# Attention values on TensorE moved from the end of a slot to directly behind the transposed scores

## What is computed

```
# layer 0 (cross): adaptive layer norm of x and of the context
q = xq @ Wq + bq ;  k, v = split(xkv @ Wkv + bkv)
x = x + softmax(q k^T / 4) v @ Wp + bp
# layer 1 (self)
h = layer_norm(x) * (1 + scale_msa) + shift_msa
x = x + (mha(h) @ self_o_w + self_o_b) * gate_msa
# layer 2 (cross), keys and values of the raw context
x = x + mha(layer_norm(x) @ q_w + q_b, context) @ cross_o_w + cross_o_b
# MLP
h = layer_norm(x) * (1 + scale_mlp) + shift_mlp
x = x + (gelu(h @ mlp_w1 + mlp_b1) @ mlp_w2 + mlp_b2) * gate_mlp
```

## Time and profile before

| | |
|---|---|
| median of 3 runs | 520.54 us |
| the profiled execution | 521.28 us |
| its span on the core, first to last instruction | 519.5 us |
| mean granted TensorE clock | 0.930 of 2.4 GHz |
| busy share PE, DVE, ACT, POOL | 85%, 56%, 48%, 35% |

### The profile page before, as it was taken

The page is one execution under the profiler, slowest core; times in us unless marked ns, Lnnn a source line. Parts: engine busy times, 40 slices in busy tenths (PEclk is TensorE's granted clock), DMA queues, the critical chain, the costliest instruction groups (busy, mean ns, idle before and its releaser), DMA issues.

```text
span 519.5 us, 11670 instructions
## 1 busy us (share of the span) xinstructions
PE 441.9 (85%) x4306; PEld 314.7 (61%) x4306; DVE 293.0 (56%) x784; ACT 249.5 (48%) x555; POOL 183.2 (35%) x245
## 2 busy tenths in 40 slices
PE   4767199888999989889697786899999998999996
PEld 3634156657576556566564553576666665689995
DVE  7648176693757565533757686556754574434321
ACT  1442147654574556445442433466666664562221
POOL 3343033463345345516214314235243422252200
PEclk9968589998899999989987997799999998999999
DMA  7899934295425188936817205238456241200000
GB/s 216 195 132 168 161 78 117 67 188 99 54 62 113 33 127 126 123 89 78 98 51 94 55 3 137 89 84 105 85 81 102 58 88 48 73 3 18 20 18 19
DMA packets 48927, 46.13 MB, mean 89 GB/s; under 512 B 12767, under 2 KB 47071, under 8 KB 48871
## 3 DMA queue, kind: packets, MB, share of 16 engines
q1 hardware_dynamic: 45951, 45.12, 47.1%
q10 hardware_dynamic: 2920, 0.27, 0.5%
HBM read 14.57 MB, written 0.93 MB: 30 GB/s over the span
## 4 chain that ended last, share of the span: by engine, by line
PE 58%; DVE 18%; issue 8%; DMA 6%; ACT 5%; POOL 3%; SPq 2%; ACTq 0%; DVEq 0%; POOLq 0%
DVE nmax L940 9%; PE bank L451 7%; PE bank L593 7%; PE bank L573 6%; PE bank L459 6%; PE bank L556 6%; PE bank L644 5%; PE bank L485 5%; PE bank L633 5%; DMA q_stack_all<-nm_t 3%; PE bank L618 3%; DVE xn L841 2%; ACT prob L785 2%; PE bank L508 2%; PE bank L468 1%
## 5 line engine op out<-in xcount | busy, mean ns | idle before, releaser
L940 DVE TENSOR_REDUCE nmax<-bank 112x1 f32<-112x375 f32 (+1 forms) x288 | 141.8, 547 | 88.1 <-PE bank L556 86.7
L785 ACT ACTIVATE prob<-bank 128x448 f32<-128x448 f32 (+2 forms) x224 | 113.4, 544 | 76.3 <-PE bank L573 72.1
L556 PE MATMUL bank<-k_stack,q_stack_all 96*128 96x375 bf16 x256 | 67.2, 342 | 14.9 <-DVE nmax L940 6.4
L573 PE MATMUL bank<-q_stack_all,k_stack 99*128 99x112 bf16 x768 | 56.4, 218 | 14.4 <-DMA q_stack_all<-nm_t 14.3
L1079 POOL TENSOR_TENSOR fill_space<-fill_space 128x375 f32<-128x375 f32 x32 | 30.2, 946 | 105.6 <-ACT fill_space L717 105.6
L573 PEld LDWEIGHTS bank<-q_stack_all,k_stack 99*128 99x128 bf16 x768 | 42.1, 100 | 32.2 <-DMA q_stack_all<-nm_t 15.1
L593 PE MATMUL bank<-prob,v_tokens 128*17 128x112 f32 (+1 forms) x1536 | 57.5, 267 | 0.1
L1093 POOL TENSOR_TENSOR v_tokens<-v_tokens,bias_rows_v 128x256 f32<-128x256 f32 (+1 forms) x48 | 33.4, 711 | 57.9 <-ACT v_tokens L729 57.7
L556 PEld LDWEIGHTS bank<-k_stack,q_stack_all 96*128 96x128 bf16 x256 | 24.3, 101 | 48.3 <-DVE nmax L940 26.4
L451 PE MATMUL bank<-fill_space,wkv 128*128 128x375 f32 x128 | 51.0, 527 | 1.7 <-ACT fill_space L738 1.7
L459 PE MATMUL bank<-wkv,fill_space 128*128 128x256 f32 (+1 forms) x192 | 48.5, 389 | 2.4 <-DVE v_all L911 1.6
(11 more groups left out here) (120 smaller groups left out, 676.2 us busy)
## 6 DMA issues: line engine op xcount, KB each, us to landing
k_stack<-fill_space SPq DMA_DIRECT2D x192, 93.8 KB, 3.7
q_stack_all<-q_part SPq DMA_DIRECT2D x72, 112.0 KB, 4.1
k_stack_all<-ctx_norm SPq DMA_DIRECT2D x24, 112.0 KB, 5.4
k_stack_all<-in_L_xcond_mlp_w_dram SPq DMA_DIRECT2D x2, 1024.0 KB, 7.1
k_stack_all<-in_L_xcond_ada_w_dram SPq DMA_DIRECT2D x1, 1536.0 KB, 16.6
ctx_tokens<-in_ctx_dram SPq DMA_DIRECT2D x2, 512.0 KB
fill_space<-gate_rows SPq DMA_DIRECT2D x2, 448.0 KB, 3.6
fill_space<-gate_rows SPq DMA_DIRECT2D x1, 896.0 KB, 5.2
```

The source lines that it names most:

```text
L556: last = pe.matmul(to[:, o:o + w], q_all[0:DEEP, q + h * N2:q + h * N2 + P], keys, start=True, stop=True)
L573: last = pe.matmul(bank[SCORE_T[n % 2]][:, j * T:(j + 1) * T], keys, q_all[0:AUG, q + h * N2:q + h * N2 + T], start=True, stop=True)
L785: act.activation(prob[n % 4][0:rows, :], bank[SCORE_T[n % 2]][0:rows, 0:GH * T], ACT.Exp).then_inc(exp_done, 1)
L940: dve.tensor_reduce(nmax[:, g * hs:(g + 1) * hs], bank[SCORE[n % 3]][0:T, 0:hs * w].rearrange("t (h k) -> t h k", k=w), AX_X, ALU.max, neg ...
```

## The change

In `tensor`, the loop of PE over slots issues the values directly behind the transposed scores and the steps last. Nothing is added or removed, and no other engine's program changes.

```
                 for u in units:
                     pe_scores_t(pe, a, u)
+                if v > 0:
+                    for u in (v - 2, v - 1):
+                        pe_values(pe, a, u)
                 for u in (v, v + 1):
                     for step in STEPS.get((a, u), ()):
                         pe_step(pe, step)
-                if v > 0:
-                    for u in (v - 2, v - 1):
-                        pe_values(pe, a, u)
```

## The result

The changed kernel takes 528.22 us, the median of 4 runs (526.37 to 528.74), against 520.58 us for the kernel before, run beside it (4 runs, 518.55 to 522.02). The ratio is 1.0148 with a 95% interval of 1.011 to 1.0186: 1.5% slower, 7.6 us. The forecast was 527.6. The profiled execution of the changed kernel took 528.58 us, its span is 526.8 us at a mean granted clock of 0.935; before it was 521.28, 519.5 and 0.930.

A forecast was written before the change was run, and what follows sets the result against it. PE, busy for 85% of the span, was taken to bound the kernel. Terms 6.3 + 2.7 + 0.5 - 3.7 + 1.3 = +7.1 us on 521.28 gave 528.4, or 527.6 on the median's scale; range 519.5 to 533.

The forecast's parts named there:

- Term 1: Ends of cross items: values 11 wait for exponential 11 behind T's copy; nine exposed ends at 0.70 us, +6.3 us.
- term 4: Given back: values moved into existing PE waits, in items 1 to 3, 5, 6, 22 and 23; -3.7 us together.
- Term 2: Start of next item: tail transposes L606 wait for ACT's `pv_sb` copy, 0.22 or about 0.4 us each; +2.7 us.
- term 3: Start of item 8: PE waits for the maxima's DMA, whose N step stands one pair later; +0.5 us.
- Term 5: Self items: output projection L618 now comes behind values 3, which wait for exponential 3; gains and losses sum to +1.3 us.
- (a): Rival: ends cost less, first layer's swallowed by DVE's chain, item 22 avoids the slow clock; 523.0 us, chance 0.20.
- (b): Rival: not slower, as five clock falls in items 6, 9, 11, 16 and 22 go; 518.6 us, chance 0.10.
- (c): Rival: much slower, the clock falls at three to nine item ends, 1.8 us each; 533 to 544 us, chance 0.10.

The follow-up runs named there:

- the control: The kernel before, PE's order unchanged, with step T of place 10 put at place 11, so ACT does exponential 11 before T's copy: 526.62 us, ratio 1.0102.
- after again: A second profiled execution of the changed kernel, with nothing altered: 529.56 us.
- both repairs: Changed kernel with T of place 10 at place 11 and `pv_sb` ahead of the last place's steps on ACT: 521.51 us; self items in old order: 521.19.

## Why the prediction was right, step by step

**Term 1, the ends.** The mechanism is shown. Values 11 wait for exponential 11, which stands behind the copy of the first T; the version with the last slots alone has it, changing ACT's order removes it (2.49), and the control turns its sign. The size was 0.80 instead of 0.70 an end. The wait itself was placed to 0.05 us (values 11 at 2.55 behind scores 10, forecast 2.50); the other 0.05 is in values 11 and the second T, 0.70 against 0.65. In the first layer the wait is 0.87, longer by its longer copy (0.18), but before, the second T waited 0.24 us there, and the end of item 0 is 3.43 instead of 2.64: 0.79 more, so that this cancels as worked out. Item 4's end, which I had as hidden, shows the same 0.79; the wait for keys behind it gives that back (2.08 before, 1.26 now), and of the pair of term 4 only 0.15 is left to see in item 5 (0.22 longer, against 0.37 with the last slots alone).

**Term 2, `pv_sb`.** The mechanism is shown by moving that copy alone, and the term was undersized: 0.43 to 0.46 us an item in the last layer instead of 0.22, and in the first layer 0.50 in item 1 (L606 at 81.33, the scores at 79.94, against 0.89 before) and 0.60 in items 2, 4, 5 and 6 instead of 0.4. 0.21 of it lies between the end of `pv_sb` (408.14) and the start of L606 (408.35). I had set that distance at 0.05, as between an exponential and its values. The version with the last slots alone holds terms 1 and 2 (the N step of term 3 stands in an earlier slot). Its cross items are 11.1 us longer where I had 9.0, although items 6 and 7 are 0.3 and 0.8 shorter there, with no fall of the clock in item 6.

**Term 3, item 8's start.** Item 7 is 0.83 and 0.77 longer, forecast 0.5. PE at its end still waits for the DMA of the maxima:

```profile
249.56 0.66 PE L573 MATMUL bank<-q_stack_all,k_stack_all 99*128 99x112 bf16 x8 [0.56 <-DMA q_stack_all<-nm_t]
```

From the N step to these scores it is 4.96 us before and 4.95 now, so item 8 starts as late as N does, as forecast, and the wait of 0.51 us ahead of values 11, which I hadn't put there, lies inside that time and costs nothing. But N stands 0.83 us later in its item (20.71 to 21.54), not 0.51. A fall of the clock reaches 2.4 us into item 7 before and 2.9 now; whether that is the rest wasn't tested.

**Term 4, given back.** The cross items are together 6.8 and 8.0 us longer in the two executions of the changed kernel, and 11.1 longer with the last slots alone. So all the rest of the change gives -4.3 and -3.1, where my terms 3 and 4 make -3.2, but its places were partly others. In item 1 I foresaw no wait ahead of the last S and a smaller one ahead of N. The changed kernel shows them almost as they were in the earlier trace rows:

```profile
90.01 0.79 PE L556 MATMUL bank<-k_stack,q_stack_all 96*128 96x375 bf16 x2 [0.34 <-DVE nmax L940]
...
94.70 0.21 PE L524 MATMUL bank<-ident_bf,nparts 112*128 112x112 bf16 x1 [0.68 <-DVE nparts L952]
```

Item 1 is 0.67 longer and the pair's gain is still in it, since with the last slots alone it is 1.30 longer: -0.63 where I had -0.51. That the waits nonetheless stay, where the pair was to fill them, is not due to the late L606: with `pv_sb` moved, L606 is on time and the two waits are 0.35 and 0.68 us all the same. The late L606 only sets where N stands, 14.76 us behind the item's start and 14.24 with `pv_sb` moved. The pair shows behind N: the next scores start 0.05 us behind it instead of 0.65. Which wait it filled no bracket shows. What I missed is slot 2 of the last layer, 0.38 us in items 17 to 20 that each have a wait hidden inside a merged row of S. Item 23 gave 0.49, forecast 0.34. Item 22 gave 0.93 in one execution and lost 0.62 in the other; its clock decides, not the pair: the falls there are 6.8 and 3.5 us long in the two executions of the kernel before, 3.4 and 6.9 in those of the changed one. Item 6, where I had -0.4 to -0.5, is 0.05 and 0.13 longer. Items 2 and 3 differ by 1.7 us between the two executions of the kernel before (51.16 and 52.84), so what the pair gave there isn't shown.

**Term 5, self items.** +1.3 was forecast, +1.56 (after again) and +1.75 (self items alone) were measured. The +3.7 of the first profile holds a fall of the clock in item 8 that the second does not have. The windows of the first and of the second profile of the changed kernel, in item 8:

```profile
249.90:253.30 3.40, 3.40 (x37) 3.17 (x38) 2.56 (x6) 1.35 (x4) 0.00 (x0) 0.50 1.10 123
```

```profile
249.90:253.30 3.40, 2.51 (x39) 2.05 (x40) 0.84 (x2) 2.15 (x5) 0.00 (x0) 1.00 1.13 125
```

The waits stand where they were put, in item 8 and, at about 1 us, in item 10:

```profile
255.06 0.39 PE L593 MATMUL bank<-prob,v_all 112*17 112x112 f32 x8 [0.56 <-ACT prob L785]
...
275.89 0.39 PE L593 MATMUL bank<-prob,v_all 112*17 112x112 f32 x8 [0.99 <-ACT prob L785]
```

Single items are off all the same. With self items alone, item 8 has +0.20 (forecast 0.8), 9 -0.02 (-0.4), 10 +0.60 (1.1), 11 -0.41 (-0.8), and 12 to 15 together +1.38 (0.6).

So the term's sum is near, but its size isn't shown. The +1.56 and the +1.75 both hold item 13's +1.19 with a fall of the clock that the kernel before doesn't have there. And with the old order in the self items these take between 77.49 and 80.97 us in seven profiles, the two of the kernel before among them. What can be set down to the order are items 8, 10 and 11, which come out alike wherever the falls are alike: together +0.39, forecast +1.1.

**The sum.** The forecast was 9.5 - 3.7 + 1.3 = +7.1, the medians have +7.6 with an interval of 5.7 to 9.7. The profiles are coarser. The cross items were to be 9.5 - 3.7 = 5.8 longer; against the first execution of the kernel before they are 6.8 and 8.0 longer, against the second, which has a longer fall of the clock in items 2 and 3 and one in item 5, 4.2 and 5.4. The runs with the last slots alone (10.1 to 14.6 where I had 8.2) say that the ends and `pv_sb` together were too small in the forecast, and something else was given back for it. That the total came out within 1 us is in part luck.

**The rivals.** (a) needed the ends of the first layer to be swallowed and the fall in item 22 to go away, (b) five falls to go away. The ends of items 0, 1, 3, 4 and 5 are each 0.78 or 0.79 us longer, and falls stand in items 6, 9, 11, 22 and at the start of item 16 in both profiles of the changed kernel. (c) was that the clock falls at the ends. Each end of items 16 to 20 now has its 0.69 us of waiting between T steps, and from 335.2 to 447.9 us the clock stays up; a stretch of items 19 and 20:

```profile
393.00:409.00 16.00, 15.03 (x192) 10.60 (x191) 8.52 (x22) 10.72 (x25) 6.02 (x8) 1.00 0.60 105
```

The Trainium skill, "TensorE: Matmul & The Clock Gate", Part 4, says that a transpose doesn't count as busy for the clock the way another matmul does. Read as the prediction read it for (c), the clock would have fallen here; the trace shows a granted clock of 1.00.

**What stays open.** Four versions that put PE ahead in the first layer (all slots but the last two, both repairs with and without self items, slots up to 6) should have been 2 to 5 us faster and are level with the kernel before. In the three of them with an undisturbed profile item 5 is 3.0 to 3.1 longer, with the clock at its lower level. It isn't the only place: with all slots but the last two and with the slots up to 6, the self items in their old order are 3.3 and 3.5 us longer. But they are 2.6 us longer in the control too, which doesn't put PE ahead. Whether the longer wait for keys brings the fall in item 5 is not settled. Over all 14 profiles, the four waits of 2.41 to 2.87 us each had a fall that began within 0.5 us of their end, and one of them is in the other execution of the kernel before (2.44 us, the fall from 186.9 to 190.4). Of the ten waits up to 2.34 us, among them that of 2.08, one had a fall, that of 2.18. An earlier issue of the DMAs to `k_stack` would tell; it wasn't tried.

## What to carry over

Two in-order engines that feed each other want the same order of work. Here, moving a step on PE past another cost nothing on PE that the runs show, and 0.8 us an end because ACT still served the old order; the cure was to move one copy on ACT for each of the two waits, and the first of these moves was a fault where PE's order had not changed. So before turning a loop round, write down for each moved pair what the other engine does between its two inputs, above all in the last turn, where the work that used to cover the wait has run out. A gain in front of a wait for a DMA can end as a longer wait: look for the next such wait behind the place before counting it. And compare two profiles only over items in which the clock fell in neither, or for as long in both; here falls moved items with no change in their order by up to 2 us.

## What was not expected of the hardware

An instruction that has waited for a semaphore starts at different distances behind its releaser: values 11 start 0.05 us after the exponential's end (406.28 to 406.33), L606 0.21 us after that of `pv_sb` (408.14 to 408.35), and the profile calls the second "issue". What makes the difference wasn't tested.

The clock differs between executions of one and the same kernel: a fall of 3.4 us at 249.9 in one and none in the other, and the 12 executions of the version with `pv_sb` moved lie between 521.48 and 530.14 us at mean clocks between 0.947 and 0.922. One profile is good to 0.02 us for most items without a fall (twice one was off by 0.12 and 0.15), and to some 3 us for the whole.

A merged row of the timeline can hold a wait: two S matmuls took 0.63 us from the row's start to the next row's and 0.33 with a pair of values ahead of them, without a bracket in either.
